# A feed-forward block with ternary weights on eight cores: a third weight buffer in the gate/up stage, and the quantising of the down stage placed between its matmuls

## The chip, the cores and the metric

One Trainium2 chip, all eight of its cores. Each core runs the same program on its own share of the rows; nothing is exchanged between cores. The metric is the device time of the slowest core in microseconds. Engines are TensorE (PE in the profile; PEld is its weight load), VectorE (DVE), ScalarE (ACT), GpSimd (POOL) and the sync engine (SP), which here only issues DMAs; DMAs are also issued from ScalarE's and GpSimd's queues (ACTq, POOLq, SPq).

## The reference

One layer: attention, then a feed-forward block whose weights are rounded to -1, 0, 1 times a scale and whose activations are rounded to 8 bits per row. The change is in the feed-forward block:

```python
def _quant_weight(w):
    scale = jnp.mean(jnp.abs(w)) + EPS
    return jnp.clip(jnp.round(w / scale), -1.0, 1.0) * scale
def _quant_act(x):
    scale = jnp.maximum(jnp.max(jnp.abs(x), axis=-1, keepdims=True), EPS) / 127.0
    return jnp.clip(jnp.round(x / scale), -128.0, 127.0) * scale
gate = jax.nn.sigmoid(bitlinear(x, w_gate))
up = bitlinear(x, w_up)
return bitlinear(gate * up, w_down)
# bitlinear(x, w) = _quant_act(x) @ _quant_weight(w).T
# x: 2 x 4096 rows of 2048; w_gate, w_up: 8192 x 2048; w_down: 2048 x 8192
x = _layernorm(x + attention(x))
x = _layernorm(x + ffn(x))
```

## The kernel before

Each core holds 1024 rows of x as 8 slots of 128 rows (`tt`, SLOTS = 8). Stages follow one another with a barrier between them: keys and values with the sums for the weight scales, queries, attention (in which gate and up weights are also made ternary), output projection and first normalisation, gate/up, down, second normalisation.

**Gate/up stage (L1311 to L1476).** The 8192 hidden columns are worked in 16 chunks (`c`) of 512. `emit_wload(c)` (L1341) puts two blocks on the sync queue: 16 transposing DMAs of a gate weight part into `wTg(c)` and 16 of the up weight into `wTu(c)`, each 128x512. `_dbuf(..., n=2)` gives two buffers, and chunk c+2 is loaded after the matmuls of chunk c (`chunk_mm`). For each slot TensorE does 32 matmuls into `gps` and `ups` (L1390, L1393; four buffers, freed by `pfree`), VectorE scales the gate half (`sgb`, L1404), ScalarE takes the sigmoid, VectorE forms `hb` (L1429) and a running maximum, GpSimd's queue stores the hidden values to `hscr`. Between `sgb` and `hb` of every second slot `emit_tern` (L858) puts one tile of the down weight through the ternary quantiser: a 1 MB load into `wfstb`, on the sync queue for even tiles and on ScalarE's for odd ones (L865), two VectorE operations (L875, L879) and a store on GpSimd's queue. So each chunk has four quantiser tiles, two of them loaded from the sync queue.

Engines work through their instructions in the order in which they are written; the order on every queue is that of the Python code.

**Down stage (L1478 to L1654).** The 8192 hidden columns are worked in 8 groups (`gidx`) of 1024. A group has two parts. First each slot is quantised: `hst` is loaded on ScalarE's queue (L1516), ScalarE takes Sign and Abs with the row's scale (L1525, L1527), VectorE adds 0.5 (`h32b`, L1537), casts to integer and back (L1540, L1542), compares, subtracts and multiplies by the sign (`h32a`, `h32b`, `hqb`; L1544, L1547, L1553), TensorE transposes eight 128x128 blocks (L1565), VectorE copies them to `hqT` (L1579). Then each slot has one burst of 32 matmuls (8 blocks of the hidden axis by 4 of the output) into `dn6` (L1628), and VectorE adds the result to `acc6` in four operations (L1643 in the first group, L1647 after). `dn6` is one buffer: a burst waits for the accumulation before it (`dn_ev`). `hqT` is one buffer, `wdT`, the down weight, has two, filled by eight transposing DMAs a group on the sync queue (L1592, L1603) after the matmuls of two groups earlier.

Of the kernel before, what the change touches and what calls it, by code (L numbers as in the profile page):

```python
# [9 lines left out]
F32 = mybir.dt.float32  # L10
I32 = mybir.dt.int32
# [44 lines left out]
def build_nc(cfg, upto=99, dbg=()):  # L56
# [68 lines left out]
    SP["w5st"] = [Sem(nc, st, "w5q%d" % q) for q in range(4)]  # L125
# [1185 lines left out]
    if upto >= 5:  # L1311
# [3 lines left out]
        wTg = _dbuf(p5, nc, "wTg", DC * 512, BF16)  # L1315
        wTu = _dbuf(p5, nc, "wTu", DC * 512, BF16)
# [19 lines left out]
        with nc.Block() as B:  # L1336
# [5 lines left out]
            def emit_wload(c):  # L1342
                @B.sync
                def _(s, c=c):
                    th = (c + 1) * tpc - 1
                    s.wait_ge(SP["tfw"][th % 2].h, fac_wb[th])
                    s.wait_ge(SP["tfw"][(th - 1) % 2].h, fac_wb[th - 1])
                    if c >= 2:
                        s.wait_ge(SM["tMM"].h, chunk_mm[c - 2])
                    for j in range(DC):  # L1350
                        SP["w5st"][c % 2].inc(s.dma_start(
                            wTg(c)[:, j * 512:(j + 1) * 512],
                            wg_q.ap()[c * 512:(c + 1) * 512,
                                      j * 128:(j + 1) * 128],
                            transpose=True), 16)

                @B.sync
                def _(s, c=c):
# [3 lines left out]
                    if c >= 2:  # L1362
                        s.wait_ge(SM["tMM"].h, chunk_mm[c - 2])
                    for j in range(DC):
                        SP["w5st"][2 + c % 2].inc(s.dma_start(
# [4 lines left out]
                w_ready[c] = (SP["w5st"][c % 2].n, SP["w5st"][2 + c % 2].n)  # L1370

            emit_wload(0)
            emit_wload(1)
            for c in range(FFC):
                for tt in range(SLOTS):
# [3 lines left out]
                    def _(te, c=c, tt=tt, n_g=n_g):  # L1379
                        if tt == 0:  # L1380
                            te.wait_ge(SP["w5st"][c % 2].h, w_ready[c][0])
                            te.wait_ge(SP["w5st"][2 + c % 2].h, w_ready[c][1])
# [65 lines left out]
                if c + 2 < FFC:  # L1448
                    emit_wload(c + 2)
# [31 lines left out]
    if upto >= 6:  # L1481
# [6 lines left out]
        h32a = p6.enter_context(nc.sbuf_tensor("h32a", [128, 1024], F32))  # L1488
        h32b = p6.enter_context(nc.sbuf_tensor("h32b", [128, 1024], F32))
        h32c = p6.enter_context(nc.sbuf_tensor("h32c", [128, 1024], F32))  # L1490
        h32i = p6.enter_context(nc.sbuf_tensor("h32i", [128, 1024], I32))
        sg6 = p6.enter_context(nc.sbuf_tensor("sg6", [128, 1024], BF16))
        hqb = _dbuf(p6, nc, "hqb", 1024, BF16)
# [6 lines left out]
        with nc.Block() as B:  # L1500
            grp_mm_last = []
            for gidx in range(NGR):
                ffb = gidx * 1024
                hq_tr = []
                for tt in range(SLOTS):
                    n_h = gidx * SLOTS + tt

                    @B.scalar
                    def _(sc, gidx=gidx, tt=tt, n_h=n_h, ffb=ffb):
                        if n_h == 0:  # L1510
                            sc.wait_ge(SP["hwr"][0].h, hwr_tot[0])
                            sc.wait_ge(SP["hwr"][1].h, hwr_tot[1])
                        if n_h >= 2:
                            sc.wait_ge(SM["vMi"].h, hq_q.get(n_h - 2, 0))
                            sc.wait_ge(SM["sEx"].h, hq_sg.get(n_h - 2, 0))
                        hq_dma[n_h] = SP["hst6"][n_h % 2].inc(sc.dma_start(  # L1516
                            hst6(n_h),
                            hscr.ap()[tt * 128:(tt + 1) * 128, ffb:ffb + 1024]), 16)

                    @B.scalar  # L1520
                    def _(sc, tt=tt, n_h=n_h):
                        sc.wait_ge(SP["hst6"][n_h % 2].h, hq_dma[n_h])
                        if n_h >= 1:
                            sc.wait_ge(SM["vMi"].h, hq_bf.get(n_h - 1, 0))
                        sc.activation(sg6[:, :], hst6(n_h), AF.Sign,  # L1525
                                      bias=0.0, scale=1.0)
                        hq_sg[n_h] = SM["sEx"].inc(sc.activation(  # L1527
                            h32a[:, :], hst6(n_h), AF.Abs, bias=0.0,
                            scale=scl["r_h"][:, tt:tt + 1]))
                    habs_done = SM["sEx"].n  # L1530

                    @B.vector
                    def _(v, tt=tt, n_h=n_h, habs_done=habs_done):
                        v.wait_ge(SM["sEx"].h, habs_done)
                        if n_h >= 2:
                            v.wait_ge(SM["tXT"].h, hq_tr_mark.get(n_h - 2, 0))
                        SM["vCh"].inc(v.tensor_scalar(h32b[:, :], h32a[:, :], 0.5,  # L1537
                                                      None, OP.add))
                        v.wait_ge(SM["vCh"].h, SM["vCh"].n)
                        SM["vCh"].inc(v.tensor_copy(h32i[:, :], h32b[:, :]))  # L1540
                        v.wait_ge(SM["vCh"].h, SM["vCh"].n)
                        SM["vCh"].inc(v.tensor_copy(h32c[:, :], h32i[:, :]))  # L1542
                        v.wait_ge(SM["vCh"].h, SM["vCh"].n)
                        SM["vCh"].inc(v.tensor_tensor(h32a[:, :], h32c[:, :],  # L1544
                                                      h32b[:, :], OP.is_gt))
                        v.wait_ge(SM["vCh"].h, SM["vCh"].n)
                        hq_q[n_h] = SM["vMi"].inc(v.tensor_tensor(  # L1547
                            h32b[:, :], h32c[:, :], h32a[:, :], OP.subtract))

                    @B.vector  # L1550
                    def _(v, n_h=n_h):
                        v.wait_ge(SM["vMi"].h, hq_q[n_h])
                        hq_bf[n_h] = SM["vMi"].inc(v.tensor_tensor(  # L1553
                            hqb(n_h), h32b[:, :], sg6[:, :], OP.mult))

                    @B.tensor
                    def _(te, gidx=gidx, tt=tt, n_h=n_h):
                        te.wait_ge(SM["vMi"].h, hq_bf[n_h])
                        if gidx > 0 and tt == 0:
                            te.wait_ge(SM["tMM"].h, grp_mm_last[gidx - 1])  # L1560
                        for j in range(8):
                            bank = (tpa6, tpb6)[(j // 8) % 2]
                            if j % 8 == 0:
                                te.wait_ge(SM["sEv"].h, bank_free.get(id(bank), 0))
                            ins = te.transpose(bank[:, (j % 8) * 128:(j % 8 + 1) * 128],  # L1565
                                               hqb(n_h)[:, j * 128:(j + 1) * 128],
                                               ident[:, :])
                            if j == 7:
# [228 lines left out]
```

## Time and profile before

| | us |
|---|---|
| median of 2 runs | 6861.18 (6858.22 to 6864.15) |
| profiled execution, its own time | 6869.79 |
| span of its slowest core (core 0), first to last instruction | 6868.2 |
| spans of the eight cores | 6800.0 to 6868.2 |
| mean granted TensorE clock, core 0 | 0.681 |
| busy over the span: PE, DVE, ACT, POOL | 45%, 44%, 21%, 6% |
| first gate/up weight load issued | 4071.0 |
| last accumulation of the down stage starts | 6759.5 |

Times inside the profile are counted from the start of the span. A "row" of a timeline merges like instructions that follow one another: start, length in us, engine, line, operation, output and inputs, count, and in brackets how long the engine had been idle and what ended that. "Granted clock" is the TensorE clock as a share of 2.4 GHz; 0.50 is the lower level, 1.2 GHz.

### The profile page before, as it was taken

How to read it: one execution, taken by the hardware profiler on the slowest of the kernel's cores; microseconds unless marked ns; L12 is line 12 of the kernel's file. 1: busy time of each engine (PE TensorE's matmuls, PEld its weight loads, DVE VectorE, ACT ScalarE, POOL GpSimd, SP SyncE). 2: the span in 40 equal slices, each digit the busy share in tenths (PEclk: the TensorE clock that was granted, in tenths of full speed). 3: DMA queues.
4: the chain of work that ended last, by engine and by line, in shares of the span. 5: the costliest groups of instructions: out<-in, count | busy, mean ns of one | idle time of the engine just before them, and what ended most of it. 6: DMA issues, size and time to landing. Idle time of an engine off the chain costs nothing. (4 is left out here: it accounts for less than half of the span.)

```text
span 6868.2 us, 49057 instructions; the slowest of 8 cores (6800.0 to 6868.2 us)
## 1 busy us (share of the span) xinstructions
PE 3084.2 (45%) x14189; PEld 1468.9 (21%) x14445; DVE 3035.8 (44%) x4630; ACT 1447.7 (21%) x2398; POOL 386.6 (6%) x747
## 2 busy tenths in 40 slices
PE   0014443143323445555546208777777444444442
PEld 0001111011112223333332103333333111112121
DVE  0015554365776555545440433433343544444443
ACT  0002222121233333333320221211111211111112
POOL 0001110111100000000000000000000000000000
PEclk9997766566655555555558558887778677777776
DMA  9976773768654333222224225656666522222202
GB/s 104 110 97 99 101 101 50 99 100 118 154 184 150 125 112 101 93 91 83 83 64 113 78 71 148 159 153 150 154 157 162 139 52 49 52 49 49 49 19 98
DMA packets 735828, 708.00 MB, mean 103 GB/s; under 512 B 607312, under 2 KB 607312, under 8 KB 705616
## 3 DMA queue, kind: packets, MB, share of 16 engines
q0 software_dynamic: 94768, 276.88, 21.1%
q1 hardware_dynamic: 580640, 268.57, 17.9%
q10 hardware_dynamic: 60160, 159.40, 7.4%
q8 instruction: 123, 2.02, 0.1%
q14 instruction: 137, 1.12, 0.1%
HBM read 545.28 MB, written 201.33 MB: 109 GB/s over the span
## 5 line engine op out<-in xcount | busy, mean ns | idle before, releaser
L1390 PE MATMUL gps<-wTg,xqTf 128*128 128x512 bf16 x1966 | 806.4, 410 | 278.4 <-DVE hb L1429 278.3
L1393 PE MATMUL ups<-wTu,xqTf 128*128 128x512 bf16 x2048 | 839.5, 410 | 56.7 <-DMA wTu<-wu_q 46.4
L950 PE MATMUL avp<-ptb,vsb 128*128 128x128 bf16 x2304 | 336.5, 300 | 707.7 <-DVE ptb L940 707.7
L1628 PE MATMUL dn<-wdT,hqT 128*128 128x512 bf16 x2000 | 509.5, 415 | 182.4 <-DVE acc L1647 146.0
L398 DVE TENSOR_REDUCE asum<-mstage 128x1 f32<-128x1024 bf16 x384 | 450.9, 1214 | 266.2 <-DMA mstage<-wg 78.0
L940 DVE COPY ptb<-ptp 128x512 bf16<-128x512 bf16 x576 | 243.5, 423 | 599.1 <-PE ptp L926 599.1
L465 PE MATMUL kps<-wkT,xtg 128*128 128x512 bf16 x491 | 222.3, 453 | 473.7 <-DMA xtg<-xkv_bf 473.5
L926 PE MATMUL ptp<-ident,pnb 128*128 128x128 bf16 x2304 | 360.2, 310 | 135.8 <-DVE pnb L1028 134.1
L999 ACT ACT_TABLE_LOAD x128 | 164.2, 1283 | 1183.4 <-remote 823.5
L1415 ACT ACT_TABLE_LOAD x128 | 164.2, 1283 | 1101.0 <-DVE sgb L1404 1101.0
L950 PEld LDWEIGHTS avp<-ptb,vsb 128*128 128x128 bf16 x2304 | 199.8, 127 | 844.4 <-issue 844.4
L1647 DVE SCALAR_TENSOR_TENSOR acc<-dn,shd,acc 128x512 f32<-128x512 f32 x224 | 152.7, 744 | 466.4 <-PE dn L1628 466.4
L1390 PEld LDWEIGHTS gps<-wTg,xqTf 128*128 128x128 bf16 x2048 | 212.7, 104 | 620.5 <-issue 475.0
L875 DVE TENSOR_SCALAR pnb3b<-wfstb,wsc 128x2048 bf16<-128x2048 f32 x64 | 82.2, 1284 | 583.9 <-DMA wfstb<-wd 583.9
L1565 PE MATMUL tpa<-ident,hqb 128*128 128x128 bf16 x512 | 64.7, 307 | 612.1 <-DVE hqb L1553 612.1
L1628 PEld LDWEIGHTS dn<-wdT,hqT 128*128 128x128 bf16 x2048 | 210.9, 105 | 479.2 <-issue 289.0
L879 DVE SCALAR_TENSOR_TENSOR tbuf5a<-wfsta,wsc,pnb3a 128x2048 bf16<-128x2048 f32 x128 | 301.0, 2352 | 13.4
L981 PE MATMUL sps<-kf,qf 128*128 128x512 bf16 x497 | 262.9, 617 | 95.2 <-ACT psb L999 65.2
L1525 ACT ACT_TABLE_LOAD x64 | 82.1, 1283 | 1047.1 <-DVE hqb L1553 1001.6
L999 ACT ACTIVATE psb<-sps,negM 128x512 bf16<-128x512 f32 x448 | 302.0, 689 | 1.3
L926 PEld LDWEIGHTS ptp<-ident,pnb 128*128 128x128 bf16 x2304 | 258.1, 145 | 205.0 <-issue 205.0
L1393 PEld LDWEIGHTS ups<-wTu,xqTf 128*128 128x128 bf16 x2048 | 212.4, 104 | 277.8 <-issue 131.7
(224 smaller groups left out, 4203.3 us busy)
## 6 DMA issues: line engine op xcount, KB each, us to landing
mstage<-wg POOLq DMA_DIRECT2D x128, 256.0 KB, 6.2
mstage<-wu POOLq DMA_DIRECT2D x128, 256.0 KB, 6.2
mstage<-wd POOLq DMA_DIRECT2D x128, 256.0 KB, 5.3
wfsta<-wg SPq DMA_DIRECT2D x32, 1024.0 KB, 6.3
wfsta<-wg ACTq DMA_DIRECT2D x32, 1024.0 KB, 7.2
wg_q<-tbuf5a POOLq DMA_DIRECT2D x64, 512.0 KB, 6.4
wfsta<-wu SPq DMA_DIRECT2D x32, 1024.0 KB, 5.9
wfsta<-wu ACTq DMA_DIRECT2D x32, 1024.0 KB, 5.1
```

The lines of the kernel that those rows point to most:

```text
L398: mt_red[t] = SM["vMi"].inc(v.reduce_sum(asum[:, t:t + 1], mstage(t)[:, 0:cw], AX.X, apply_absolute_value=True))
L465: te.matmul(kslice, lhs, wkT[:, j * KV:(j + 1) * KV], start=(j == 0), stop=False)
L879: fac_mark[t] = SM["vMi"].inc(v.scalar_tensor_tensor(tbuf5(t)[:, 0:cw], wfst(t)[:, 0:cw], wsc[:, ti:ti + 1], pnb3[:, 0:cw], OP.is_ge, OP.add))
L926: last = te.transpose(ptp[:, gpar * 1024 + b * 128: gpar * 1024 + (b + 1) * 128], pnb(u)[:, (grp * 4 + b) * 128: (grp * 4 + b + 1) * 128], ...
L940: pte_marks.append(SM["vMi"].inc(v.tensor_copy(ptb(gpar)[:, :], ptp[:, gpar * 1024:gpar * 1024 + 512])))
L950: last = te.matmul(avp[:, (u % 2) * 512:(u % 2) * 512 + 128], vsb[:, kb * KV + kvh * HD: kb * KV + kvh * HD + HD], ptb(gpar)[:, b * 128:(b ...
L981: SM["tMM"].inc(te.matmul(sps[:, (gc % 4) * 512:(gc % 4) * 512 + 512], qf[:, u * 128:(u + 1) * 128], kf[:, kvh * S + cch * 512: kvh * S + ...
L999: chunk_exp.append(SM["sEx"].inc(sc.activation(dst(u)[:, cch * 512:(cch + 1) * 512], sps[:, (gc % 4) * 512:(gc % 4) * 512 + 512], AF.Exp, ...
L1390: te.matmul(gps[:, qo:qo + 512], lhs, wTg(c)[:, j * 512:(j + 1) * 512], start=(j == 0), stop=(j == DC - 1))
L1393: last = te.matmul(ups[:, qo:qo + 512], lhs, wTu(c)[:, j * 512:(j + 1) * 512], start=(j == 0), stop=(j == DC - 1))
L1415: sg_done[n_g] = SM["sEx"].inc(sc.activation(sg2[:, :], sgb[:, :], AF.Sigmoid, bias=0.0, scale=1.0))
L1628: last = te.matmul(dn6[:, oc2 * 512:(oc2 + 1) * 512], lhs, wdT(gidx)[:, cf8 * D + oc2 * 512: cf8 * D + (oc2 + 1) * 512], start=(cf8 == 0), ...
```

## The change

Gate/up: `wTg` and `wTu` get three buffers instead of two, with six semaphores instead of four. Three chunks are loaded ahead of the loop, and chunk c+3 is loaded after the matmuls of chunk c.

Down: the quantising of a slot is a function, `emit_hq(gidx, tt)`. The eight slots of group 0 are quantised ahead; after that, slot tt of group g+1 is quantised behind burst and accumulation of slot tt of group g. The two casts go from VectorE to ScalarE (`sc.copy`). `hqT` has two buffers, `hqb` one instead of two; the transposes alternate between the PSUM tiles `tpa6` and `tpb6`. The down weight's loads are one function, `emit_wdload`, with the same waits. Four working tiles lie on the other side of the memory.

```diff
-            emit_wload(0)
-            emit_wload(1)
+            for c0 in range(min(3, FFC)):
+                emit_wload(c0)
...
-                    if c >= 2:
-                        s.wait_ge(SM["tMM"].h, chunk_mm[c - 2])
+                    if c >= 3:
+                        s.wait_ge(SM["tMM"].h, chunk_mm[c - 3])
...
-                if c + 2 < FFC:
-                    emit_wload(c + 2)
+                if c + 3 < FFC:
+                    emit_wload(c + 3)
...
-        hqT = p6.enter_context(nc.sbuf_tensor("hqT", [128, 8 * NTOK], BF16))
+        hqT = _dbuf(p6, nc, "hqT", 8 * NTOK, BF16)
...
-        hqb = _dbuf(p6, nc, "hqb", 1024, BF16)
+        hqb = p6.enter_context(nc.sbuf_tensor("hqb", [128, 1024], BF16))
...
+                @B.vector
+                def _(v, n_h=n_h):
+                    v.wait_ge(SM["sEx"].h, hq_sg[n_h])
+                    if n_h >= 1:
+                        v.wait_ge(SM["sEx"].h, hq_cp.get(n_h - 1, 0))
+                    hq_ts[n_h] = SM["vCh"].inc(v.tensor_scalar(
+                        h32b[:, :], h32a[:, :], 0.5, None, OP.add))
+
+                @B.scalar
+                def _(sc, n_h=n_h):
+                    sc.wait_ge(SM["vCh"].h, hq_ts[n_h])
+                    if n_h >= 1:
+                        sc.wait_ge(SM["vMi"].h, hq_q.get(n_h - 1, 0))
+                    SM["sEx"].inc(sc.copy(h32i[:, :], h32b[:, :]))
+                    sc.wait_ge(SM["sEx"].h, SM["sEx"].n)
+                    hq_cp[n_h] = SM["sEx"].inc(sc.copy(h32c[:, :], h32i[:, :]))
+
+                @B.vector
+                def _(v, n_h=n_h):
+                    v.wait_ge(SM["sEx"].h, hq_cp[n_h])
+                    if n_h >= 1:
+                        v.wait_ge(SM["tXT"].h, hq_tr_mark.get(n_h - 1, 0))
...
+            wd_ready = {0: emit_wdload(0)}
+            for tt in range(SLOTS):
+                emit_hq(0, tt)
+            if NGR > 1:
+                wd_ready[1] = emit_wdload(1)
...
+                    if gidx + 1 < NGR:
+                        emit_hq(gidx + 1, tt)
                 grp_mm_last.append(SM["tMM"].n)
+                if gidx + 2 < NGR:
+                    wd_ready[gidx + 2] = emit_wdload(gidx + 2)
```

What stands in a row on the queues. The sync queue at the start of the gate/up stage, before: two chunks' weight loads, then the first two quantiser loads.

```order
L1351 DMA_TRANSPOSE wTg<-wg_q 128x512 x16
L1357 UNCONDITIONAL_BRANCH
L1365 DMA_TRANSPOSE wTu<-wu_q 128x512 x16
L861 UNCONDITIONAL_BRANCH
L865 DMA wfstb<-wd 128x2048
L861 UNCONDITIONAL_BRANCH
L865 DMA wfstb<-wd 128x2048
```

This is the second chunk's load; the third chunk's comes behind the two quantiser loads. The same queue in the changed kernel, from the second chunk's load on.

```order
L1351 DMA_TRANSPOSE wTg<-wg_q 128x512 x16
L1357 UNCONDITIONAL_BRANCH
L1365 DMA_TRANSPOSE wTu<-wu_q 128x512 x16
L1343 UNCONDITIONAL_BRANCH
L1351 DMA_TRANSPOSE wTg<-wg_q 128x512 x16
L1357 UNCONDITIONAL_BRANCH
L1365 DMA_TRANSPOSE wTu<-wu_q 128x512 x16
L861 UNCONDITIONAL_BRANCH
L865 DMA wfstb<-wd 128x2048
```

The third chunk's block has moved ahead of the first quantiser loads; everywhere after, one block of 32 and two quantiser loads alternate as before. VectorE in the down stage, before, where the last slot of group 0 is quantised and its accumulations begin.

```order
L1540 CAST h32i<-h32b 128x1024
L1542 CAST h32c<-h32i 128x1024
L1544 TENSOR_TENSOR h32a<-h32c,h32b 128x1024
L1547 TENSOR_TENSOR h32b<-h32c,h32a 128x1024
L1550 UNCONDITIONAL_BRANCH
L1553 TENSOR_TENSOR hqb<-h32b,sg6 128x1024
L1573 UNCONDITIONAL_BRANCH
L1579 COPY hqT<-tpa6 128x8x128
L1635 UNCONDITIONAL_BRANCH
L1643 TENSOR_SCALAR acc6<-dn6,shd 128x512 x4
L1635 UNCONDITIONAL_BRANCH
L1643 TENSOR_SCALAR acc6<-dn6,shd 128x512 x4
```

VectorE at the same place in the changed kernel.

```order
L1583 COPY hqT<-tpb6 128x8x128
L1636 UNCONDITIONAL_BRANCH
L1644 TENSOR_SCALAR acc6<-dn6,shd 128x512 x4
L1531 UNCONDITIONAL_BRANCH
L1536 TENSOR_SCALAR h32b<-h32a 128x1024
L1548 UNCONDITIONAL_BRANCH
L1553 TENSOR_TENSOR h32a<-h32c,h32b 128x1024
L1556 TENSOR_TENSOR h32b<-h32c,h32a 128x1024
L1559 TENSOR_TENSOR hqb<-h32b,sg6 128x1024
L1577 UNCONDITIONAL_BRANCH
L1583 COPY hqT<-tpa6 128x8x128
L1636 UNCONDITIONAL_BRANCH
```

Accumulation and quantising now alternate slot by slot, and the two casts are gone from VectorE. TensorE in the same stretch of the changed kernel: a burst, the transposes of the next group's slot, the next burst.

```order
L1629 MATMUL dn6<-wdT,hqT 128x512 x32
L1562 UNCONDITIONAL_BRANCH
L1570 MATMUL tpb6<-ident,hqb 128x128 x8
L1617 UNCONDITIONAL_BRANCH
L1629 MATMUL dn6<-wdT,hqT 128x512 x32
```

Before, eight sets of transposes and eight bursts stood in two separate rows. ScalarE in the changed kernel, one slot and the head of the next.

```order
L1516 DMA hst6<-hscr 128x1024
L1520 UNCONDITIONAL_BRANCH
L1525 ACTIVATE sg6<-hst6 128x1024
L1527 ACTIVATE h32a<-hst6,r_h 128x1024
L1539 UNCONDITIONAL_BRANCH
L1544 CAST h32i<-h32b 128x1024
L1546 CAST h32c<-h32i 128x1024
L1508 UNCONDITIONAL_BRANCH
L1516 DMA hst6<-hscr 128x1024
```

The casts are a block of their own, behind Sign and Abs and ahead of the next slot's load.

## Rows read from the trace of the kernel before

**Rows 1.** The page, costliest groups: gate and up matmuls (busy, mean, idle before, releaser).

```profile
L1390 PE MATMUL gps<-wTg,xqTf 128*128 128x512 bf16 x1966 | 806.4, 410 | 278.4 <-DVE hb L1429 278.3
L1393 PE MATMUL ups<-wTu,xqTf 128*128 128x512 bf16 x2048 | 839.5, 410 | 56.7 <-DMA wTu<-wu_q 46.4
```

**Rows 2.** Timeline of the sync queue, gate/up stage (start, us, queue, line, operation).

```profile
4113.32 20.74 SPq L1351 DMA_TRANSPOSE wTg<-wg_q  x16
...
4155.46 1.00 SPq L865 DMA_DIRECT2D wfstb<-wd  x2
4192.99 23.73 SPq L1351 DMA_TRANSPOSE wTg<-wg_q  x16
...
5254.34 22.01 SPq L1351 DMA_TRANSPOSE wTg<-wg_q  x16
```

**Rows 3.** Timeline of VectorE, start and end of the gate/up stage.

```profile
4161.06 1.29 DVE L875 TENSOR_SCALAR pnb3b<-wfstb,wsc 128x2048 bf16<-128x2048 f32 x1 [29.08 <-DMA wfstb<-wd]
...
5305.73 1.29 DVE L875 TENSOR_SCALAR pnb3b<-wfstb,wsc 128x2048 bf16<-128x2048 f32 x1 [23.24 <-DMA wfstb<-wd]
...
5338.95 0.75 DVE L1404 TENSOR_SCALAR sgb<-gps,sgx 128x512 f32<-128x512 f32 x1
...
5394.86 0.75 DVE L1404 TENSOR_SCALAR sgb<-gps,sgx 128x512 f32<-128x512 f32 x1
```

**Rows 4.** Timeline of all engines, last quantising slot of group 1, down stage.

```profile
5663.46 1.13 ACT L1527 ACTIVATE h32a<-hst,r_h 128x1024 f32<-128x1024 f32 x1
5664.77 0.69 DVE L1537 TENSOR_SCALAR h32b<-h32a 128x1024 f32<-128x1024 f32 x1 [1.58 <-ACT h32a L1527]
...
5667.16 1.22 DVE L1544 TENSOR_TENSOR h32a<-h32c,h32b 128x1024 f32<-128x1024 f32 x1
...
5669.81 1.23 DVE L1553 TENSOR_TENSOR hqb<-h32b,sg 128x1024 bf16<-128x1024 f32 x1
5671.12 1.28 ACT L1525 ACT_TABLE_LOAD   x1 [6.52 <-DVE hqb L1553]
...
5671.29 1.01 PE L1565 MATMUL tpa<-ident,hqb 128*128 128x128 bf16 x8 [8.90 <-DVE hqb L1553]
...
5673.84 6.34 PE L1628 MATMUL dn<-wdT,hqT 128*128 128x512 bf16 x16 [1.53 <-DVE hqT L1579]
```

**Rows 5.** Timeline of TensorE: first bursts of groups 0 and 7, a warm one.

```profile
5507.03 9.36 PE L1628 MATMUL dn<-wdT,hqT 128*128 128x512 bf16 x31 [1.52 <-DVE hqT L1579]
...
5708.05 7.07 PE L1628 MATMUL dn<-wdT,hqT 128*128 128x512 bf16 x31 [2.98 <-DVE acc L1647]
...
6675.94 8.60 PE L1628 MATMUL dn<-wdT,hqT 128*128 128x512 bf16 x31 [1.53 <-DVE hqT L1579]
```

**Rows 6.** Timeline of VectorE: accumulations, the operation behind one, the last.

```profile
5715.22 2.73 DVE L1647 SCALAR_TENSOR_TENSOR acc<-dn,shd,acc 128x512 f32<-128x512 f32 x4 [7.32 <-PE dn L1628]
...
5926.81 2.73 DVE L1647 SCALAR_TENSOR_TENSOR acc<-dn,shd,acc 128x512 f32<-128x512 f32 x4 [7.32 <-PE dn L1628]
5929.45 0.68 DVE L1537 TENSOR_SCALAR h32b<-h32a 128x1024 f32<-128x1024 f32 x1
...
6759.48 2.73 DVE L1647 SCALAR_TENSOR_TENSOR acc<-dn,shd,acc 128x512 f32<-128x512 f32 x4 [7.32 <-PE dn L1628]
```

**Rows 7.** Two stretches: length; busy PE, PEld, DVE, ACT, POOL; granted clock; DMA; GB/s.

```profile
5700.00:5750.00 50.00, 35.97 (x149) 15.06 (x150) 12.59 (x19) 0.00 (x0) 0.00 (x0) 0.93 0.00 0
...
5950.00:6000.00 50.00, 5.05 (x40) 3.87 (x40) 32.67 (x36) 16.89 (x15) 0.00 (x0) 0.50 0.27 72
```

**Rows 8.** DMA issues of `hst` from 5440 to 5460 (median to landing), and all 64.

```profile
hst<-hscr ACTq DMA_DIRECT2D x2, 512.0 KB, 7.0
...
DMA to landing us min/median/max: 3.4/3.6/11.9
```

**Rows 9.** Groups of ScalarE: loads ahead of the Copy of L529, the CAST.

```profile
L529 ACT ACT_TABLE_LOAD x32 | 41.1, 1283 | 501.2 <-PE tkp L516 501.2
...
L597 ACT CAST krow_bf<-krow 1x4 bf16<-1x4 f32 x1 | 0.2, 193 | 0.1
```

More of the change, by code:

```diff
@@ L124, in build_nc @@
     SP["mst"] = [Sem(nc, st, "mst%d" % q) for q in range(4)]
-    SP["w5st"] = [Sem(nc, st, "w5q%d" % q) for q in range(4)]
+    SP["w5st"] = [Sem(nc, st, "w5q%d" % q) for q in range(6)]
     SP["tf"] = [Sem(nc, st, "tf%d" % q) for q in range(4)]
@@ L1501, in build_nc, with emit_hq @@
             grp_mm_last = []
-            for gidx in range(NGR):
+            hq_ready, hq_ts, hq_cp = {}, {}, {}
+            def emit_hq(gidx, tt):
+                n_h = gidx * SLOTS + tt
                 ffb = gidx * 1024
[L1504 to L1568, printed above, removed]
-                                SM["tXT"].inc(ins)
-                        hq_tr_mark[n_h] = SM["tXT"].n
-                    t_mark = SM["tXT"].n
-                    @B.vector
-                    def _(v, tt=tt, t_mark=t_mark):
-                        bank = tpa6
-                        v.wait_ge(SM["tXT"].h, t_mark)
-                        dst = hqT[:].rearrange("p (j k) -> p j k", j=8) \
-                            [:, 0:8, tt * 128:(tt + 1) * 128]
-                        SM["sEv"].inc(v.tensor_copy(dst, bank[:, 0:1024]))
-                        bank_free[id(bank)] = SM["sEv"].n
-                hq_ready = SM["sEv"].n
@@ new lines, in _ @@
+                @B.scalar
+                def _(sc, tt=tt, n_h=n_h):
+                    sc.wait_ge(SP["hst6"][n_h % 2].h, hq_dma[n_h])
+                    if n_h >= 1:
+                        sc.wait_ge(SM["vMi"].h, hq_bf.get(n_h - 1, 0))
+                    sc.activation(sg6[:, :], hst6(n_h), AF.Sign,
+                                  bias=0.0, scale=1.0)
+                    hq_sg[n_h] = SM["sEx"].inc(sc.activation(
+                        h32a[:, :], hst6(n_h), AF.Abs, bias=0.0,
+                        scale=scl["r_h"][:, tt:tt + 1]))
@@ new lines, in _ @@
+                @B.tensor
+                def _(te, gidx=gidx, tt=tt, n_h=n_h):
+                    te.wait_ge(SM["vMi"].h, hq_bf[n_h])
+                    if gidx >= 2 and tt == 0:
+                        te.wait_ge(SM["tMM"].h, grp_mm_last[gidx - 2])
+                    bank = (tpa6, tpb6)[n_h % 2]
+                    te.wait_ge(SM["sEv"].h, bank_free.get(id(bank), 0))
+                    for j in range(8):
+                        ins = te.transpose(bank[:, j * 128:(j + 1) * 128],
+                                           hqb[:, j * 128:(j + 1) * 128],
+                                           ident[:, :])
+                    SM["tXT"].inc(ins)
+                    hq_tr_mark[n_h] = SM["tXT"].n
@@ new lines, in emit_hq, with _ @@
+                t_mark = SM["tXT"].n
+                @B.vector
+                def _(v, gidx=gidx, tt=tt, n_h=n_h, t_mark=t_mark):
+                    bank = (tpa6, tpb6)[n_h % 2]
+                    v.wait_ge(SM["tXT"].h, t_mark)
+                    dst = hqT(gidx).rearrange("p (j k) -> p j k", j=8) \
+                        [:, 0:8, tt * 128:(tt + 1) * 128]
+                    SM["sEv"].inc(v.tensor_copy(dst, bank[:, 0:1024]))
+                    bank_free[id(bank)] = SM["sEv"].n
+                if tt == SLOTS - 1:
+                    hq_ready[gidx] = SM["sEv"].n
@@ L1590, in _ @@
                         s.wait_ge(SM["tMM"].h, grp_mm_last[gidx - 2])
-                    for cf8 in range(4):
+                    for cf8 in range(8):
                         SP["wd6"][gidx % 2].inc(s.dma_start(
@@ L1596, in _ @@
                             transpose=True), 16)
[L1598 to L1611 removed]
+                return SP["wd6"][gidx % 2].n
+            wd_ready = {0: emit_wdload(0)}
[3 more added lines that the diff above has]
+                wd_ready[1] = emit_wdload(1)
+            assert NOC <= 4
+            for gidx in range(NGR):
                 for tt in range(SLOTS):
```

73 lines of the change are left out of this document (41 added, 32 removed).

## The prediction

> **What bounds the kernel now.** I read the page first, then the timeline of the sync queue in the gate/up stage, then timelines of all engines in the down stage. The chain that ended last only shows the output stage, which the change leaves alone, so each stage is read from its own loop.
>
> *Gate/up stage.* TensorE stands before the gate matmuls for 278 us on VectorE's `hb`, and for weights only once, 46 us, on the first load [rows 1]. VectorE in its turn stands on the load of a quantiser tile: 23.24 us before the one at 5305.73 [rows 3]. The reader is to see why in the sync queue [rows 2]: a block of 32 transposing loads (gate and up of one chunk) keeps the queue some 42 to 45 us, and the two quantiser loads of the next chunk stand behind it. The block itself waits for the end of a chunk's matmuls. So the stage runs in a ring: chunk ends, 45 us of block, quantiser load, VectorE catches up, chunk ends. From the block at 4192.99 to that at 5254.34 are 13 rounds, 81.64 us each. A chunk whose loads have no block ahead takes 55.9 us: `sgb` of the same slot in the last two chunks, 5338.95 to 5394.86 [rows 3].
>
> *Down stage.* Eight quantising slots, then eight matmul slots, and so on; neither kind of work lies beside the other. From the first burst of group 0 (5507.03) to that of group 7 (6675.94) are 56 slot pairs, 20.87 us each [rows 5]. A warm burst is 7.07 us long and VectorE starts on the result 0.10 later [rows 5, 6].
>
> *The clock.* In the quantising stretch 5950 to 6000 the granted clock is 0.50, the lower level (1.2 GHz); in 5700 to 5750, bursts with 3 us between them, it is 0.93, nearly all at 2.4 GHz [rows 7]. The first burst after a quantising phase starts at the lower level: 9.36 us in group 0, 8.60 in group 7, mean of the eight 9.19 against 7.07 warm [rows 5].
>
> **The change part by part.** Durations are from the profiled execution: span 6868.2 us, time 6869.8, which is 8.6 above the median 6861.2. I work out a difference and put it on the median.
>
> *Third weight buffer.* Loading chunk c+3 at the end of chunk c waits for the same matmuls, stands at the same place and holds the same 32 transposes as loading c+2 did. The ring keeps its 81.6 us. Two things change. Before the first two quantiser loads there are now three blocks instead of two: 4113.32 to 4155.46 is 42.1 us for one [rows 2], and VectorE has been waiting 29 us for that load when it comes [rows 3], so nothing hides it: +42.1. At the end one more chunk has no block ahead of it: 81.6 - 55.9 = -25.7. Sum +16.4 us. Lower bound: the first block beside running matmuls costs nothing, -26; upper bound: the last chunks gain nothing because of the quantiser loads on ScalarE's queue, +42. I take the sum, since both halves are read from rows.
>
> *Down stage, interleaved.* In the new order TensorE has burst(tt), transposes of the next group's slot tt, burst(tt+1); VectorE has accumulate(tt), `h32b`, comparison, subtraction, product, copy of the transposes. The product needs the whole quantising chain, the chain starts on VectorE behind the accumulate, the accumulate needs burst(tt), and burst(tt+1) is queued on TensorE behind the transposes, which need the product. So the two kinds of work still run one after the other. Only Sign, Abs, their table load, the `hst` load and the copy to `hqT` go beside the burst. One slot pair is then, start to start:
> - burst start to accumulate start, after a pause: 9.19 + 0.10 = 9.29 [rows 5, 6]
> - accumulate to `h32b`: 5926.81 to 5929.45 = 2.64 [rows 6]
> - `h32b` (0.69) to the first cast, now on ScalarE: 0.77, the 0.07 being what ScalarE takes behind `hqb` (5669.81 + 1.23 to 5671.12) [rows 4]
> - first to second cast: 1.18. The trace has no ScalarE cast of this size. Nearest is ScalarE's Abs over the same elements, 1.13 [rows 4], plus some 0.05 for the wait on itself; below, a cast at VectorE's speed 0.8; above, 1.3
> - second cast to comparison: 1.28, as Abs to `h32b`, 5663.46 to 5664.77 = 1.31, less 0.03 [rows 4]
> - comparison to product 2.65 (5667.16 to 5669.81), product to the transposes 1.48 (to 5671.29) [rows 4]
> - transposes to the next burst: 0.90, since eight take 1.01 with overlapping ends [rows 4]
>
> Sum 20.2 us. Before, the two casts cost VectorE 2.39 from `h32b` to comparison (5664.77 to 5667.16); now it is 3.23, so the move to ScalarE costs 0.84 on the path, because nothing on VectorE may pass them. Over 56 pairs: 56 x 20.2 = 1131. At each of seven group changes the burst needs the last copy to `hqT`: 2.55 (5671.29 to the burst at 5673.84) instead of 0.90, 7 x 1.65 = 12. Sum 1143 against 1168.9: -26 us.
>
> The Trainium skill (page "ScalarE: Activation LUTs", section Rules for kernel authors) advises keeping plain arithmetic on VectorE as the faster engine; here Abs at 1.13 beside a 0.69 `h32b` agrees, and by it the move of the casts is a loss, which the 0.84 already holds.
>
> *Head of the down stage.* The first eight slots have no burst to lie beside: 8 x 0.84 = +7. The `hst` load of a slot now stands on ScalarE behind the casts of the slot before, so it is issued 5.2 us ahead of its use (1.28 to the comparison, 2.65 to the product, 1.31 to the table load) instead of a whole slot ahead. It lands in 3.6 us as a rule, but in 7.0 beside the transposing loads [rows 8]; some five of the eight are beside them, 1.3 to 1.8 late each: +7. Together +14; bounds 0 and +40 (11.9 at worst [rows 8]). Later in the stage the `hst` load has over 10 us to spare, the weight loads keep their place and wait, and the second `hqT` and the one `hqb` are no wait, as the order is serial anyway. The last group is bursts alone, as before: 86 us to the last accumulate at 6759.48 [rows 6].
>
> Sum: +16 - 26 + 14 = +4 us. Forecast 6865 us, no change that can be told: about 2%, 137 us, is what a measurement of this kernel tells from none.
>
> **The rivals.**
>
> *A table load before each pair of casts.* Every block of ScalarE's that begins with an ACTIVATE has one, even the plain Copy of line 529, 32 blocks and 32 loads of 1.28 us; the one CAST, of line 597, stands in a block that had a load anyway [rows 9]. If the compiler puts one ahead of the casts, 64 x 1.28 = +82: 6947 us. Against it: in the program it is another instruction than ACTIVATE. The Trainium skill (page "ScalarE: Activation LUTs", section Table sets: the hidden batching unit) says that the compiler puts a load before every activation that needs one, which would spare a cast; no row here shows it. Chance 0.13.
>
> *Slower: the bursts run at the lower clock throughout.* Between any two bursts TensorE now stands some 10 us with 1 us of transposes in the stretch, which is how it stands in the quantising stretch where the clock is 0.50 [rows 7]. If the clock never rises within a burst, it is twice 7.07 = 14 us, +4.8 for each of 56: +270, 7135 us. It decides as soon as a burst after such a pause averages 11.7 us (56 x 2.4 = 134). For it: every burst is now such a one. Against: all eight first bursts of a group, after the same pause, rose to the higher clock on their way. The Trainium skill (page "TensorE: Matmul & The Clock Gate", section Loop structure matters more than you think) warns of just this loop, a long wait between matmuls after which they run cold; by it the time would be this rival's, and the first bursts at 9.2 agree only in part. Chance 0.06.
>
> *The bursts stay warm.* 7.07 instead of 9.19: 56 x 2.1 = -119, 6746 us. Against: no burst after a quantising slot did. Chance 0.05.
>
> *The change does what the buffers suggest.* If the third weight buffer took away VectorE's waits, 14 chunks would gain 25.7 each, -360; if the quantising lay under the bursts, the slot would fall to some 13 us, -400. Either gives about 6500 or less. Against: weights are waited for once [rows 1], and the order on VectorE and TensorE above. Chance 0.03.
>
> **How the numbers follow.** The forecast has 0.73. Its own range: burst mean 8.6 to 10 us (-39 to +40), casts 0.8 to 1.3 each (-43 to +13), head -14 to +26, gate/up -42 to +26, which do not all fall to one side: 6800 to 6930. To leave no more than 2 in 10 out I reach over the table loads: 6790 to 6955. Faster by over 2%: the last rival and a little of the one before, 0.05. Slower: the cold bursts and table loads with slow casts, 0.07. Within: 0.88.
>
> **What would show it.** First quantiser load of the gate/up stage about 42 us later on the sync queue, at 4197 to 4198; blocks still 81 to 82 us apart; two chunks of 56 us at the end; the stage about 16 us longer. In the down stage starts of bursts 20.2 us apart, granted clock there near 0.7, TensorE waiting about 10 us for `hqb` before each set of transposes, ScalarE casts of about 1.05 us without a table load. It is wrong if bursts average over 11 or under 8 us, if blocks come closer than 80 us, or if the transposes do not wait for `hqb`.

## The result and the profile after

The changed kernel takes 6907.7 us (median of 11 runs, 6891.0 to 6944.3), the kernel before 6858.4 in the same sessions: ratio 1.0076, 95% interval 1.0059 to 1.0093. That is within 2% and within the range, but 49 us slower where +4 was forecast. One more run of 15312 us is left out of the median: six of its cores took 8590 us or more, where the other two took 6865 and 6915. The profiled execution took 6927.0 us, span 6925.3 on core 0.

On core 0 of the two profiles the 57 us between the spans come apart like this: the stages before gate/up, whose code is the same, +24.9 (first weight load at 4095.9 instead of 4071.0; +7 on the mean of all eight cores); gate/up +7.5 (eight cores: +11); down +27.4 (eight cores: +29); output stage -3 (eight cores: 0). The code changed in gate/up and down, and the down stage is where the forecast was off.

The sync queue of the changed kernel, gate/up stage (start, length, queue, line, operation), beside [rows 2]:

```profile
4137.75 20.70 SPq L1351 DMA_TRANSPOSE wTg<-wg_q  x16
...
4180.71 20.70 SPq L1351 DMA_TRANSPOSE wTg<-wg_q  x16
4201.56 20.70 SPq L1365 DMA_TRANSPOSE wTu<-wu_q  x16
4222.37 0.98 SPq L865 DMA_DIRECT2D wfstb<-wd  x2
4257.39 22.95 SPq L1351 DMA_TRANSPOSE wTg<-wg_q  x16
...
5224.33 25.23 SPq L1351 DMA_TRANSPOSE wTg<-wg_q  x16
```

The first quantiser load stands 126.5 us after the first weight load at 4095.90, where it stood 84.4 after it before: the third block is 42 us and nothing hides it. From 4257.39 to 5224.33 are 12 rounds of 80.6 us: the ring is as it was. The gate and up matmuls in the page's costliest groups, beside [rows 1]:

```profile
L1390 PE MATMUL gps<-wTg,xqTf 128*128 128x512 bf16 x1966 | 780.0, 397 | 332.9 <-DVE hb L1429 332.2
L1393 PE MATMUL ups<-wTu,xqTf 128*128 128x512 bf16 x2048 | 810.7, 396 | 52.2 <-DMA wTu<-wu_q 46.0
```

TensorE waits for weights once, 46 us, as before. It waits for VectorE 54 us longer, but by the same rows the matmuls of the two lines are busy 55 us less, so the longer wait is not a longer stage. The end of the stage on VectorE, the same slot of the last three chunks, beside [rows 3]:

```profile
5313.79 0.75 DVE L1404 TENSOR_SCALAR sgb<-gps,sgx 128x512 f32<-128x512 f32 x1
...
5371.05 0.75 DVE L1404 TENSOR_SCALAR sgb<-gps,sgx 128x512 f32<-128x512 f32 x1
...
5427.40 0.75 DVE L1404 TENSOR_SCALAR sgb<-gps,sgx 128x512 f32<-128x512 f32 x1
```

Two chunks of 57.3 and 56.4 us, as read from the one before (55.9).

One slot pair of the down stage on all engines, in the middle of a group (PEld rows left out), which answers to [rows 4 to 6]:

```profile
6000.37 8.26 PE L1629 MATMUL dn<-wdT,hqT 128*128 128x512 bf16 x31
...
6008.74 2.72 DVE L1648 SCALAR_TENSOR_TENSOR acc<-dn,shd,acc 128x512 f32<-128x512 f32 x4 [7.37 <-PE dn L1629]
6011.38 0.68 DVE L1536 TENSOR_SCALAR h32b<-h32a 128x1024 f32<-128x1024 f32 x1
6012.20 1.28 ACT L1544 ACT_TABLE_LOAD   x1 [9.42 <-DVE h32b L1536]
6013.49 1.04 ACT L1544 CAST h32i<-h32b 128x1024 int32<-128x1024 f32 x1
6014.62 1.04 ACT L1546 CAST h32c<-h32i 128x1024 f32<-128x1024 int32 x1
...
6015.84 1.22 DVE L1553 TENSOR_TENSOR h32a<-h32c,h32b 128x1024 f32<-128x1024 f32 x1 [3.77 <-ACT h32c L1546]
...
6018.49 1.22 DVE L1559 TENSOR_TENSOR hqb<-h32b,sg 128x1024 bf16<-128x1024 f32 x1
...
6019.98 1.01 PE L1570 MATMUL tpb<-ident,hqb 128*128 128x128 bf16 x8 [11.34 <-DVE hqb L1559]
6020.78 8.30 PE L1629 MATMUL dn<-wdT,hqT 128*128 128x512 bf16 x31
```

Read it downwards: each row starts where the one above ends, whatever the engine. That is the serial ring, burst to burst 20.41 us. The row nobody wants is the table load at 6012.20, between `h32b` and the casts. ScalarE's groups in the down stage:

```profile
L1525 ACT ACT_TABLE_LOAD x64 | 82.1, 1283 | 289.4 <-DVE hqb L1559 248.6 <-DMA hst<-hscr 40.8
L1544 ACT ACT_TABLE_LOAD x64 | 82.1, 1283 | 562.1 <-DVE h32b L1536 562.1
...
L1544 ACT CAST h32i<-h32b 128x1024 int32<-128x1024 f32 x64 | 66.8, 1044 | 0.7
```

So the compiler did put a load ahead of all 64 pairs of casts. By themselves these are 82 us. Part of that came back in the bursts: over the 56 bursts with quantising between them the mean from start to accumulation is 8.57 us on core 0 (8.63 on the mean of the eight cores) instead of the 9.29 forecast. All means of bursts below are counted this way, from the first matmul to the start of VectorE's accumulation; a row of the timeline is 0.1 us shorter, since it ends with the matmuls.

### The profile page after: what moved, and what is told of

Its sections match the earlier page's. It is cut to its first block and busy times, and to the rows that moved or that the text cites. A ratio compares the mean times of both kernels' runs of the same rounds, so it can differ in the third digit from the quotient of the medians.

```text
span 6925.3 us, 49237 instructions; the slowest of 8 cores (6864.2 to 6925.3 us)
## 1 busy us (share of the span) xinstructions
PE 3074.2 (44%) x14187; PEld 1470.0 (21%) x14445; DVE 2942.0 (42%) x4502; ACT 1663.0 (24%) x2590; POOL 386.2 (6%) x747
## 3 DMA queue, kind: packets, MB, share of 16 engines
q8 instruction: 123, 2.02, 0.1%
## 5 line engine op out<-in xcount | busy, mean ns | idle before, releaser
L1390 PE MATMUL gps<-wTg,xqTf 128*128 128x512 bf16 x1966 | 780.0, 397 | 332.9 <-DVE hb L1429 332.2
L1393 PE MATMUL ups<-wTu,xqTf 128*128 128x512 bf16 x2048 | 810.7, 396 | 52.2 <-DMA wTu<-wu_q 46.0
L1629 PE MATMUL dn<-wdT,hqT 128*128 128x512 bf16 x1998 | 537.8, 432 | 35.4 <-DVE acc L1648 21.1
L677 PE MATMUL qps<-wT,xqT 128*128 128x512 bf16 x499 | 183.0, 543 | 130.9 <-DMA wT<-wq_bf 128.4
L467 PE MATMUL vps<-wvT,xtg 128*128 128x512 bf16 x510 | 226.2, 444 | 2.3 <-issue 1.6
```

The lines of the kernel that those rows point to most:

```text
L467: te.matmul(vslice, lhs, wvT[:, j * KV:(j + 1) * KV], start=(j == 0), stop=False)
L1390: te.matmul(gps[:, qo:qo + 512], lhs, wTg(c)[:, j * 512:(j + 1) * 512], start=(j == 0), stop=(j == DC - 1))
L1393: last = te.matmul(ups[:, qo:qo + 512], lhs, wTu(c)[:, j * 512:(j + 1) * 512], start=(j == 0), stop=(j == DC - 1))
L1629: last = te.matmul(dn6[:, oc2 * 512:(oc2 + 1) * 512], lhs, wdT(gidx)[:, cf8 * D + oc2 * 512: cf8 * D + (oc2 + 1) * 512], start=(cf8 == 0), ...
```

## The experiments

All nine ran on eight cores and are set against the kernel before in the same session (median 6851 to 6852 us). The changed kernel was not run again in these sessions; it is taken as 1.0076 of the kernel before. Means over eight cores are from the profiled execution of each kernel.

**No second block on ScalarE.** The casts stand in the block of Sign and Abs. The order of every queue is that of the changed kernel. Of the waits one is gone, ScalarE's for the subtraction of the slot before, which VectorE's own order already ensures.

```diff
-                @B.scalar
-                def _(sc, n_h=n_h):
                     sc.wait_ge(SM["vCh"].h, hq_ts[n_h])
-                    if n_h >= 1:
-                        sc.wait_ge(SM["vMi"].h, hq_q.get(n_h - 1, 0))
                     SM["sEx"].inc(sc.copy(h32i[:, :], h32b[:, :]))
```

> The changed kernel with the two casts put into the same block of ScalarE's as Sign and Abs, so that no second block begins; every wait and every order on every queue stays. Theory (the 64 table loads of 1.28 us ahead of the casts lie on the path, 56 between two bursts and 8 in the head): the table loads fall from 128 to 64 in the down stage, a slot pair from 20.9 to about 19.6 us, the time by 64 x 1.29 = 82 to about 6825 us, 0.995 of the kernel before. Rival (ScalarE has time to spare, the loads cost nothing, the loss has another cause): 6908 us, 1.008 of before.

Measured: 6852.1 us, ratio 1.0009 (0.9994 to 1.0024). ScalarE's groups in the down stage now:

```profile
L1535 ACT ACT_TABLE_LOAD x64 | 82.1, 1283 | 301.3 <-DVE hqb L1556 223.8 <-DMA hst<-hscr 77.5
...
L1541 ACT CAST h32i<-h32b 128x1024 int32<-128x1024 f32 x64 | 66.8, 1044 | 586.6 <-DVE h32b L1527 586.6
```

64 loads fewer, the casts wait for VectorE alone, and the loss against the kernel before is gone: with the load absent the change is worth nothing measurable, which is what the prediction had for it. The 6825 expected of this run was too low, though: only 0.67% of 6852 = 46 us came back by the ratios (56 by the medians of different sessions), not 82; the down stage is 44 us shorter on the mean of the eight cores. The reason stands in the bursts of this run, mean 9.24 us on core 0 instead of 8.57: 56 x 0.67 = 38 us given back. That opened the question taken up two experiments on.

**Two weight buffers, down stage as changed.**

```diff
-        wTg = _dbuf(p5, nc, "wTg", DC * 512, BF16, n=3)
+        wTg = _dbuf(p5, nc, "wTg", DC * 512, BF16, n=2)
...
-                if c + 3 < FFC:
-                    emit_wload(c + 3)
+                if c + 2 < FFC:
+                    emit_wload(c + 2)
```

> The changed kernel with the gate/up stage put back to two weight buffers; the down stage stays changed. Theory (the third buffer adds one block of 42 us ahead of the first quantiser load and saves one round of 82 against 57 us at the end): 17 us faster than the changed kernel, about 6891 us, 1.005 of before, first quantiser load 84 us after the first weight load instead of 126. Rival (the third buffer helps, weights come earlier): slower than 6908. Rival 2 (it moves nothing): 6908.

Measured: 6883.0 us, ratio 1.0051 (1.0035 to 1.0068). Against 1.0076 that is 17 us, the 16 to 17 of the sum, though the two intervals overlap. The profiles point the same way: the gate/up stage is 21 us shorter on the mean of the eight cores, and the down stage the same within 1 us. Its sync queue on core 6:

```profile
4070.40 21.17 SPq L1351 DMA_TRANSPOSE wTg<-wg_q  x16
...
4156.23 0.99 SPq L865 DMA_DIRECT2D wfstb<-wd  x2
```

The first quantiser load is back at 85.8 us after the first weight load.

**Casts back on VectorE.**

```diff
-                    SM["sEx"].inc(sc.copy(h32i[:, :], h32b[:, :]))
-                    sc.wait_ge(SM["sEx"].h, SM["sEx"].n)
-                    hq_cp[n_h] = SM["sEx"].inc(sc.copy(h32c[:, :], h32i[:, :]))
+                    v.wait_ge(SM["vCh"].h, SM["vCh"].n)
+                    SM["vCh"].inc(v.tensor_copy(h32i[:, :], h32b[:, :]))
+                    v.wait_ge(SM["vCh"].h, SM["vCh"].n)
+                    hq_ts[n_h] = SM["vCh"].inc(v.tensor_copy(
+                        h32c[:, :], h32i[:, :]))
```

> The changed kernel with the two casts back on VectorE, between the addition of 0.5 and the comparison; ScalarE has only Sign and Abs. Theory (the whole chain of burst, accumulation, quantising and transposes is serial, so each saved us counts): from the addition to the comparison 2.4 instead of 4.5 us, 64 x 2.1 = 134 less, about 6774 us, 0.988 of before. Rival (VectorE's queue is what is full, so casts on it lengthen the slot by 1.4 instead): 6908 or more.

Measured: 6775.9 us, ratio 0.9887 (0.9869 to 0.9904); the total is what the theory had. The same stretch on core 4:

```profile
6001.27 0.68 DVE L1534 TENSOR_SCALAR h32b<-h32a 128x1024 f32<-128x1024 f32 x1
6002.05 0.69 DVE L1537 CAST h32i<-h32b 128x1024 int32<-128x1024 f32 x1
6002.85 0.69 DVE L1539 CAST h32c<-h32i 128x1024 f32<-128x1024 int32 x1
6003.71 1.23 DVE L1547 TENSOR_TENSOR h32a<-h32c,h32b 128x1024 f32<-128x1024 f32 x1 [0.17 <-DVE h32c L1539]
```

2.44 us from `h32b` to the comparison instead of 4.46. The slot pair fell by a little less than these 2.02 us, on the mean of the eight cores from 20.90 to 19.14, because the bursts were 0.25 us longer (8.88 instead of 8.63). The down stage took 1242 us on that mean, where it took 1335 before and 1364 in the changed kernel. So the interleaving itself is a small gain, and the move of the casts to ScalarE turned it into a loss.

**A gap between transposes and burst.** Every burst waits for VectorE's copy of the transposes ahead of it.

```diff
-                        te.wait_ge(SM["sEv"].h, hq_ready[gidx])
+                        te.wait_ge(SM["sEv"].h, SM["sEv"].n)
```

> The changed kernel in which every burst waits for VectorE's copy of the transposes just ahead of it, as only the first burst of a group does now. This puts about 1.6 us between transposes and burst for 49 more bursts. Theory A (bursts are 8.5 instead of the 9.2 that was forecast because they follow the transposes at once): the bursts go back to some 9.4 us, as the first of each group are now, and the time rises by 49 x (1.6 + 0.9) = 122 to about 7030 us. Theory B (the length of the burst hangs on the pause before the transposes alone): bursts stay 8.5, the time rises by 49 x 1.6 = 78 to about 6986 us.

Measured: 6998.6 us, ratio 1.0217 (1.0200 to 1.0235), so +97 us against the changed kernel: between the 78 and 122 of the two theories. On core 0 the bursts had a mean of 9.32 us, one slot pair 22.7. By itself that spoke for theory A, but the kernel without table loads above had 9.24 with its transposes right ahead of the bursts. So a third theory came up, C: the length hangs on how far apart bursts start. Both edits were put together to test it.

**Gap, and no second block.** The two diffs above in one kernel.

> The kernel without the second table load (casts in the block of Sign and Abs), and every burst waiting for VectorE's copy of the transposes just ahead of it. The two before it: without the load bursts had a mean of 9.24 us on core 0 although they followed the transposes at once, in pairs of 20.2; with load and gap 9.32, in pairs of 22.7; with the load alone 8.57, settling at 8.4 in pairs of 20.45. Theory A (adjacent transposes shorten the burst): bursts 9.2 to 9.5, slot pair 11.0 + 1.3 + 9.3 = 21.6, time 6852 + 76 = about 6930 us. Theory C (the burst's length hangs on how far apart bursts start, and settles low where that is about 20.5 us, load or no load): the pair settles near 20.5 with bursts of 8.1 to 8.4, time about 6870 us.

Measured: 6885.1 us, ratio 1.0055 (1.0033 to 1.0077), which is 6874 to 6904. Theory A's 6930 is outside, and theory C's 6870 just misses it too. TensorE on core 0 in this kernel (the profiled execution was the longest of its ten, 6936 us):

```profile
5742.75 10.50 PE L1626 MATMUL dn<-wdT,hqT 128*128 128x512 bf16 x32 [1.05 <-DVE hqT L1580]
...
5765.32 8.52 PE L1626 MATMUL dn<-wdT,hqT 128*128 128x512 bf16 x32 [1.05 <-DVE hqT L1580]
...
5785.92 8.47 PE L1626 MATMUL dn<-wdT,hqT 128*128 128x512 bf16 x32 [1.05 <-DVE hqT L1580]
...
5806.55 8.39 PE L1626 MATMUL dn<-wdT,hqT 128*128 128x512 bf16 x32 [1.14 <-DVE hqT L1580]
```

and in the kernel without the load and without the gap:

```profile
5704.31 9.26 PE L1626 MATMUL dn<-wdT,hqT 128*128 128x512 bf16 x32
...
5765.03 9.62 PE L1626 MATMUL dn<-wdT,hqT 128*128 128x512 bf16 x31
...
5785.46 9.64 PE L1626 MATMUL dn<-wdT,hqT 128*128 128x512 bf16 x31
```

With the gap, a burst of 10.50 us is followed by three of 8.4 to 8.5, which start 20.6 apart. Without it the last two bursts are 9.6 long, but they too start 20.4 apart. So what the two kernels share is not the length of a burst but the length of the whole pair. From the start of an accumulation to the next burst the rest of the ring takes 12.0 us in the changed kernel and in the one with gap and no load, and 10.7 in the one without load or gap (medians of the pairs within a group, core 0). 12.0 + 8.5 and 10.7 + 9.7 both make 20.4 to 20.5. In the changed kernel the bursts of a group on core 4 run 9.4, 8.9, 8.7, then creep down to 8.4, and the pairs to 20.5.

This is a tendency, not a rule that every pair obeys. Of the 49 pairs within groups only 14 on core 0 and 27 on core 4 lay between 20.40 and 20.65 in the changed kernel; 8 and 13 without load or gap, where the others reach down to 18.4; 19 and 12 with the gap and no load, where in some groups most pairs are 21.6 to 23.3 instead. Over all 56 pairs this last kernel had bursts of 9.02 us and pairs of 21.05 on the mean of the eight cores, half way between theory A's 21.6 and theory C's 20.5. With a rest of 10.0 (casts on VectorE) or 13.3 (load and gap) no pair of core 0 came to it, and the bursts jumped between 7.7 and 10.1. That the bursts lengthened is shown, and it is why an edit of 1.28 us on the path moved the pair by only 0.67. Why they did was not isolated.

**Quantiser loads ahead of the weight block, three buffers.**

```diff
+            for t0 in (0, 2):
+                emit_qload(B, n_fac_gu + t0)
             for c0 in range(min(3, FFC)):
                 emit_wload(c0)
...
+                if c + 1 < FFC:
+                    for t0 in (0, 2):
+                        emit_qload(B, n_fac_gu + 4 * (c + 1) + t0)
                 if c + 3 < FFC:
                     emit_wload(c + 3)
```

`emit_qload` is the load of `emit_tern`, taken out of it for the even tiles.

> The changed kernel in which the two quantiser loads of the sync queue for chunk c+1 stand ahead of the block of 32 weight transposes issued at the end of chunk c, and those of chunk 0 ahead of the first block; three weight buffers. Theory (the gate/up stage is a ring: chunk end, 45 us of block, quantiser load, VectorE, chunk end): the ring is cut, VectorE no longer waits 25 us a chunk, chunks of 56 to 60 us instead of 81, the stage falls from about 1345 to some 1000 us, the time to about 6560 us, 0.957 of before. Rival (the DMA engines, busy 0.62 in that stage, are what the chunk waits for): chunks stay over 75 us, time over 6820 us.

Measured: 6627.8 us, ratio 0.9673 (0.9651 to 0.9695). The waits of core 0 in the stage (who waited for whom, us, times, longest), and one stretch of it:

```profile
DVE pnb3b L887 <- DMA wfstb<-wd: 282.6, 33, 16.8
...
PE gps L1404 <- DVE hb L1443: 62.6, 24, 6.5
```

```profile
4300.00:5000.00 700.00, 656.24 (x2949) 291.20 (x2948) 376.68 (x460) 175.98 (x184) 74.33 (x138) 0.97 0.90 208
```

The ring is cut: TensorE's wait for `hb` falls from 332 to 63 us, VectorE's waits for quantiser tiles from 592 to 283, the stage on core 0 from 1358 to 1052 (mean of the eight cores: 1343 to 1074). The time missed the 6560 of the expectation by 68 us: chunks are 60 to 62 us, not 56. One chunk on the sync queue of core 0 shows what it is held by now:

```profile
4602.21 11.71 SPq L861 DMA_DIRECT2D wfstb<-wd  x2
4614.12 26.64 SPq L1363 DMA_TRANSPOSE wTg<-wg_q  x16
4640.96 22.41 SPq L1377 DMA_TRANSPOSE wTu<-wu_q  x16
4663.47 11.73 SPq L861 DMA_DIRECT2D wfstb<-wd  x2
```

The queue is never free: 61.3 us from one pair of quantiser loads to the next. The pair took 1 us in the ring and takes 11.7 here, because the second of the two now waits for its buffer (in the code, for VectorE's work on an earlier tile), and the weight block stands behind it; the block takes 49 us in these rows instead of 45. In the stretch above the DMA share is 0.90 and TensorE is busy for 656 of 700 us; against the 56 to 57 us of a chunk with no block ahead, some 5 us a chunk are left. The rival may be right in part about the DMA engines; no run separates them from the wait on the queue.

**The same with two buffers.**

> The same with two weight buffers. Theory (a block takes 45 us and a chunk 56 to 60, so a block issued at a chunk's end is there before its successor ends, and the third buffer carries nothing): equal to the kernel with three within 15 us. Rival (with the ring cut the third buffer is needed, since weights now come late): TensorE waits for wTu each chunk, over 60 us slower than with three.

Measured: 6622.8 us, ratio 0.9660 (0.9638 to 0.9682), equal to three buffers. The third buffer gained nothing in either order.

**Quantising one slot further ahead, casts on VectorE.**

```diff
+            for n0 in range(SLOTS):
+                emit_q(n0)
+                emit_t(n0)
+            emit_q(SLOTS)
...
-                    if gidx + 1 < NGR:
-                        emit_hq(gidx + 1, tt)
+                    if n_c + SLOTS < NH6:
+                        emit_t(n_c + SLOTS)
+                    if n_c + SLOTS + 1 < NH6:
+                        emit_q(n_c + SLOTS + 1)
```

`emit_q` is the load and the chain up to the product, `emit_t` the transposes and VectorE's copy.

> The changed kernel with casts on VectorE and the quantising one slot further ahead: on TensorE burst(K), transposes of slot K+8, burst(K+1); on VectorE accumulate K, copy of the transposes K+8, quantising chain of slot K+9. The burst K+1 now waits for accumulate K only, and the chain lies beside it. Theory (the loss of the interleaving is the serial ring through TensorE's and VectorE's queues): a slot falls from 20.9 to 10.1 to 11 us, bound equally by burst plus accumulation (7.2 + 2.8) and by VectorE's 10.0, down stage from 1368 to about 770 us, time about 6310 us, 0.921 of before; granted clock there above 0.85. Rival (VectorE or ScalarE holds the slot at 15 us or more): over 6560 us.

Measured: 6326.0 us, ratio 0.9242 (0.9195 to 0.9289). One slot on core 4:

```profile
5767.05 7.07 PE L1629 MATMUL dn<-wdT,hqT 128*128 128x512 bf16 x31 [2.53 <-DVE acc L1648]
...
5772.53 1.23 DVE L1553 TENSOR_TENSOR hqb<-h32b,sg 128x1024 bf16<-128x1024 f32 x1
...
5774.01 0.61 PE L1567 MATMUL tpa<-ident,hqb 128*128 128x128 bf16 x8
...
5774.23 2.73 DVE L1648 SCALAR_TENSOR_TENSOR acc<-dn,shd,acc 128x512 f32<-128x512 f32 x4 [0.47 <-PE dn L1629]
...
5777.10 7.07 PE L1629 MATMUL dn<-wdT,hqT 128*128 128x512 bf16 x31 [2.48 <-DVE acc L1648]
```

The product of the next slot ends at 5773.8, just before the burst does, VectorE is idle for 0.47 us, and burst follows burst after 10.05 us. What TensorE waits for now is the accumulation (2.48 us), since `dn6` is one buffer. The mean of the 56 slots is 10.6 on core 4 and 11.3 on core 0, where more bursts ran at the lower clock (mean 8.4 against 7.6). The down stage is 768 and 823 us on these cores; it was 1339 and 1341 before and 1369 on both in the changed kernel. Of the 582 us between this kernel and the changed one, 132 belong to the casts on VectorE (6775.9 us above) and 450 to the one slot of shift.

**Both cures.** The last kernel with the quantiser loads moved and two weight buffers.

> Both cures in one: quantiser loads ahead of the weight block with two weight buffers (6623 us with the changed down stage), and the down stage with casts on VectorE and the quantising one slot further ahead (6326 us with the changed gate/up stage). The stages stand behind a barrier, so if each cure acts in its own stage the savings against the changed kernel's 6908 add: 285 + 582 = 867, time about 6041 us, 0.882 of before. If they share something (the clock, the order in which cores reach the memory), less: over 6080 us.

Measured: 6019.6 us, ratio 0.8785 (0.8770 to 0.8800). It beats both kernels, and the savings add within 22 us (6041 expected). The page's busy line:

```profile
PE 3023.5 (50%) x14187; PEld 1444.4 (24%) x14445; DVE 3024.7 (50%) x4630; ACT 1447.7 (24%) x2398; POOL 386.7 (6%) x747
```

TensorE and VectorE have about the busy time they had, in a span 840 us shorter.

## Why the prediction was right, and where not

The verdict, no change that 2% can tell, was right, and so was most of the working. The size was off, because two terms of the down stage missed in opposite directions, +82 and -40 us. That they cancelled by half is luck; the verdict did not need it, since the table loads alone make 6947 us, 1.3% more than before.

*Gate/up, +16.4.* Right in its parts: the block ahead of the first quantiser load 42.1 forecast, 42 measured; two free chunks at the end instead of one, 56 to 57 us each. The stage grew by only 7.5 us on core 0 and 11 on the mean of eight, because its rounds were shorter: 80.6 instead of 81.6 on core 0. Rounds scatter more than that from core to core (78.9 to 81.7 before, 79.0 to 80.6 after), so the sign "closer than 80 us" of the forecast, set from core 0 alone, could not have told anything. Taking the third buffer away gave back 17 us.

*The serial ring, 20.2 us a pair.* The mechanism is shown: the rows of one pair, the pair shorter by 1.76 us when the casts went back to VectorE, and the drop to 10.6 once the ring was cut. Term by term: accumulate to `h32b` 2.64 both; `h32b` to ScalarE 0.82 for 0.77; cast to cast 1.13 for 1.18, at the 1.04 that was bounded by 0.8 and 1.3; second cast to comparison 1.22 for 1.28; comparison to transposes 4.14 for 4.13; transposes to burst 0.80 for 0.90.

*The step that failed* is the choice among the two rows of [rows 9]: I gave the table load before the casts 0.13, since a cast is no ACTIVATE. All 64 loads are there. The rival put +82 us on it and 6947 in all; measured was +49. The difference is mostly the second mis-sized term.

*The burst after a pause, 9.29.* In the changed kernel it was 8.57 on core 0: 56 x 0.72 = 40 us less than its term. The first bursts of the groups had 9.3, as the eight first bursts before; those that followed crept down to 8.4. Taking the mean of eight bursts that each come after a whole quantising phase for bursts that repeat about every 20 us was the error. With the load gone the mean was 9.24, close to the term; no run shows which of these values another loop would have.

*The balance of the down stage on core 0.* The 56 pairs: forecast -26; table loads 56 x 1.29 = +72, shorter bursts -40, the smaller terms above 56 x -0.15 = -8, sum -2; measured 1170.6 against 1168.9, +2. Head +22, see below. The last group, bursts alone, took 87.1 us instead of 83.5, +4, where nothing was forecast. Together +27, as measured.

*Head, +14.* Measured 108.2 us instead of 85.9, so +22; ten of it are its eight table loads, and the late `hst` loads are there, two of them, 4.7 and 9.6 us in ScalarE's waits, where five short ones were forecast.

*The rivals.* Bursts at the lower clock throughout: no burst of the changed kernel was over 10.2 us, and the granted clock over the 56 pairs was 0.71. In the burst at 6000.37 the first six matmuls start 0.43 us apart and those after them 0.22. The Trainium skill (page "TensorE: Matmul & The Clock Gate", section Loop structure matters more than you think) warned of this loop; the trace agrees only that each burst starts low. Bursts warm throughout: only some of the last group's were 7.07 us. The buffers doing what they suggest: three against two, with the ring and without it, says no.

The Trainium skill (page "ScalarE: Activation LUTs", section Table sets: the hidden batching unit) has the load placed before activations that need one. Here it was also placed before a plain cast that opens a block. The trace decides: 64 of L1544 in the rows above.

## What to carry to other kernels

Interleaving two kinds of work slot by slot hides nothing when each queue holds the other's next step: before counting overlap, follow one slot through the in-order queues, and if the second matmul burst stands behind work that needs the first, shift that work by one more slot. A third buffer is worth something only if its consumer is seen waiting for the transfer; here it was a long run of DMA issues standing ahead of a small urgent load on the same queue, and moving two loads in front of it gave 4%, the third buffer nothing. The moved loads can then be what the run of issues waits behind, as the 11.7 us rows show, so the queue is to be read again afterwards. When work goes to ScalarE as a block of its own, count a table load with it until the profile shows otherwise, and put it in a block that already has one.

## What the runs showed of the hardware that was not expected

A table load of 1.28 us stood before a block of ScalarE's that holds two CASTs and no ACTIVATE, 64 times; with the casts in the block of Sign and Abs there was one load for all four.

The length of a matmul burst that comes after some 10 us of pause is not one number, and it does not follow the pause alone. Mean burst and mean pair in us, eight cores, by the rest of the ring: 8.9 and 19.1 at a rest of 10.0; 9.35 and 20.3 at 10.7; 8.6 and 20.9 at 12.05; 9.0 and 21.05 at 11.96; 9.4 and 22.8 at 13.3. In the middle three, pairs gather near 20.5 us whether the burst must be 8.4 or 9.7 for it. So a microsecond taken off the path of such a loop can come back in part only. Why it is 20.5, and why only some pairs get there, stays open.

With the ring cut, a block of 32 transposing loads took 51 us to issue on the mean instead of 45 to 46, while the DMA share was 0.90 instead of 0.62. That the fuller DMA engines are what slows the queue fits these numbers, but was not tested.
